# Eighteen places instead of ten for the feed-forward pieces between the attention groups of a unit

## The reference, cut to what matters

```
q, k = l2norm(LN(x) @ w_q), l2norm(LN(x) @ w_k);  v = x @ w_v
m    = (0.5 + 0.5 tanh(15 (q k' - 0.27))) * gate_q * gate_k      # no softmax: a sigmoid of the scores
x1   = LN(x + (m @ v) @ w_o + b_o)
h    = silu(Q(x1) @ Q(w_gate)') * (Q(x1) @ Q(w_up)')             # Q: blockwise FP4 grid, 704 columns
out  = LN(x1 + Q(h) @ Q(w_down)')
```

## Time and profile before

| | |
|---|---|
| median of 3 runs | 4472.55 us (4470.05 to 4476.02) |
| the profiled execution | 4469.53 us, its span 4467.7 us |
| PE busy / ACT busy / DVE busy | 93% / 90% / 35% of the span |
| granted TensorE clock | 0.985 of 2.4 GHz over the span, 1.00 in the main stage's stretches shown |

### The profile page before, as it was taken

One profiled execution on the slowest core, in us unless ns is written; L12 is line 12 of the kernel. 1 busy time (PEld: TensorE's weight loads), 2 busy tenths in 40 slices (PEclk: granted clock), 3 DMA queues, 4 the chain that ended last, 5 costly groups with the idle time before them and its releaser, 6 DMA issues.

```text
span 4467.7 us, 80907 instructions
## 1 busy us (share of the span) xinstructions
PE 4139.1 (93%) x28776; PEld 1293.7 (29%) x28776; DVE 1558.9 (35%) x4536; ACT 4026.8 (90%) x3275; POOL 159.2 (4%) x120
## 2 busy tenths in 40 slices
PE   7977889999999999999999999999999999999997
PEld 5651222222222222222222222222222222222223
DVE  6772013233333323332333332333233333333235
ACT  4658999999999999999999999999999999999993
POOL 2330000000000000000000000000000000000001
PEclk9989999999999999999999999999999999999998
DMA  3445433443344434443344334433444344434440
GB/s 110 125 116 83 61 61 61 76 76 60 57 75 77 64 61 67 77 67 62 63 77 70 61 62 77 77 60 61 72 77 64 63 66 76 72 57 64 77 80 14
DMA packets 180059, 315.51 MB, mean 71 GB/s; under 512 B 65265, under 2 KB 141809, under 8 KB 154609
## 3 DMA queue, kind: packets, MB, share of 16 engines
q1 hardware_dynamic: 179568, 309.41, 41.2%
HBM read 266.82 MB, written 42.47 MB: 69 GB/s over the span
## 4 chain that ended last, share of the span: by engine, by line
PE 68%; ACT 16%; issue 8%; DVE 4%; DMA 2%; SPq 2%; POOL 0%; ACTq 0%; POOLq 0%; DVEq 0%
PE ps L1213 34%; PE ps L1203 19%; ACT room L660 15%; PE ps L1240 7%; PE ps L1263 4%; DMA m_f<-fused_t 1%; DVE room L807 1%; SPq L486 1%; PE ps L1158 0%; SPq L462 0%; DVE st L761 0%; DMA vt<-v_gated 0%; DVE xnT L797 0%; PE ps L1225 0%; PE ps L1169 0%
## 5 line engine op out<-in xcount | busy, mean ns | idle before, releaser
L660 ACT ACTIVATE room<-ps 128x1024 f32<-128x1024 f32 (+1 forms) x2816 | 3792.9, 1416 | 246.2 <-PE ps L1203 231.7
L1213 PE MATMUL ps<-room,vt 128*32 128x512 f32 x16384 | 2064.4, 605 | 0.0
L1203 PE MATMUL ps<-qs,room 64*128 64x512 f16 x8198 | 1330.5, 384 | 249.5 <-ACT room L660 214.3
L1203 PEld LDWEIGHTS ps<-qs,room 64*128 64x128 f16 x8198 | 311.2, 93 | 1802.3 <-ACT room L660 1133.9
L1213 PEld LDWEIGHTS ps<-room,vt 128*32 128x32 f32 x16384 | 389.7, 109 | 954.8 <-issue 954.8
L1240 PE MATMUL ps<-wguT,m_xqT 128*128 128x352 f32 x960 | 348.2, 485 | 0.0
L905 DVE TENSOR_TENSOR vz<-ps,vz 128x352 f32<-128x352 f32 x120 | 63.0, 525 | 757.7 <-ACT vz L665 757.7
L910 DVE TENSOR_TENSOR vz<-ps,vz 128x352 f32<-128x352 f32 x120 | 63.0, 525 | 595.9 <-PE ps L1240 595.9
L1263 PE MATMUL ps<-wdnT,wqk 128*128 128x256 f32 x720 | 198.9, 404 | 0.6 <-DVE wqk L875 0.6
L1240 PEld LDWEIGHTS ps<-wguT,m_xqT 128*128 128x128 f32 x960 | 162.6, 189 | 105.2 <-issue 54.3
L561 POOL TENSOR_TENSOR m_x<-m_x,bo 128x256 f32<-128x256 f32 x60 | 43.6, 727 | 3972.7 <-DMA m_x<-in_L_attn_x_dram 3972.7
(11 more groups left out here) (165 smaller groups left out, 2211.0 us busy)
## 6 DMA issues: line engine op xcount, KB each, us to landing
room<-k_parts SPq DMA_DIRECT2D x520, 256.0 KB, 9.8
vt<-v_gated SPq DMA_DIRECT2D x65, 1024.0 KB, 17.5
qs<-q_parts SPq DMA_DIRECT2D x520, 32.0 KB, 10.4
gqb<-q_gates SPq DMA_DIRECT2D x256, 64.0 KB, 2.1
room<-in_L_attn_x_dram SPq DMA_DIRECT2D x16, 512.0 KB, 4.2
v_gated<-vz SPq DMA_DIRECT2D x64, 128.0 KB, 2.1
q_parts<-room SPq DMA_DIRECT2D x32, 256.0 KB, 2.1
k_parts<-room SPq DMA_DIRECT2D x32, 256.0 KB, 2.2
```

Source lines behind the costliest of these rows:

```text
L660: act.activation(res[:, c, o:o + m, :], ps[:, o:o + m, :], ACT.Sigmoid, scale=2 * SHARP / QK_UP ** 2, bias=-2 * SHARP * THRESH).then_inc(b ...
L1203: ins = pe.matmul(ps[:, BANK[n % 2] + i, :], ks[o:o + HROWS, par, h // 2, kt * P:(kt + 1) * P], qs[o:o + HROWS, par, h // 2, :], start=Tru ...
L1213: ins = pe.matmul(ps[32 * h:32 * h + 32, SUM_BANK, :], vt[:, par, n * HD:n * HD + 32], r, start=kt == 0, stop=kt == KT - 1, skip_group_che ...
```

## The change

The tables name eighteen places where they named ten. P becomes P0 and P1 (places 5 and 6, before 7), X moves from 19 to 18, each of G0 to G3 becomes two single products (21 and 22, 26 and 27, 30 and 31, 34 and 35, before 23, 27, 31, 35), and D0 and D1 become D0, D1, D2, D3 and D45 (9, 10, 11, 13 and 14, before 11 and 15). H0 and H1 stay. ACT's two sigmoids of the gates come behind groups 24 and 28, before 25 and 29. The waits go with the first product of what was a piece, the signals with the last one.

```diff
-BEGIN = {7: "P", 19: "X", 23: "G0", 27: "G1", 31: "G2", 35: "G3"}
-END = {0: "H0", 3: "H1", 11: "D0", 15: "D1"}
-GATE_ACT = {25: 0, 29: 1}
+BEGIN = {5: "P0", 6: "P1", 18: "X", 21: "G0", 22: "G1", 26: "G2", 27: "G3", 30: "G4", 31: "G5", 34: "G6", 35: "G7"}
+END = {0: "H0", 3: "H1", 9: "D0", 10: "D1", 11: "D2", 13: "D3", 14: "D45"}
+GATE_ACT = {24: 0, 28: 1}
...
-                if what == "P":
-                    pe.wait_ge(l_f, 16 * (k + 1))
-                    wait(pe, l_hT, 2 * k)
-                    for c in range(DC):
-                        ins = pe.matmul(c_ps[:, 0:D], m_f[:, c, :], wo[:, c, :], start=c == 0, stop=c == DC - 1)
-                    ins.then_inc(l_P, 1)
+                if what[0] == "P":
+                    c = int(what[1])
+                    if c == 0:
+                        pe.wait_ge(l_f, 16 * (k + 1))
+                        wait(pe, l_hT, 2 * k)
+                    ins = pe.matmul(c_ps[:, 0:D], m_f[:, c, :], wo[:, c, :], start=c == 0, stop=c == DC - 1)
+                    if c == DC - 1:
+                        ins.then_inc(l_P, 1)
...
-                    p = int(what[1])
-                    if p == 0:
+                    p, c = divmod(int(what[1]), DC)
+                    if p == 0 and c == 0:
                         pe.wait_ge(l_xT, k + 1)
-                    else:
+                    elif c == 0:
                         pe.wait_ge(l_ge, 4 * k + p)
-                    for c in range(DC):
-                        ins = pe.matmul(c_ps[:, 0:FH], m_xqT[:, c, :], wguT[:, c, p * FH:(p + 1) * FH],
-                                        start=c == 0, stop=c == DC - 1)
-                    ins.then_inc(l_G, 1)
+                    ins = pe.matmul(c_ps[:, 0:FH], m_xqT[:, c, :], wguT[:, c, p * FH:(p + 1) * FH],
+                                    start=c == 0, stop=c == DC - 1)
+                    if c == DC - 1:
+                        ins.then_inc(l_G, 1)
...
-                    half = int(what[1])
-                    if half == 0:
+                    steps = [int(i) for i in what[1:]]
+                    if steps[0] == 0:
                         pe.wait_ge(l_hT, 2 * k + 2)
...
-                    for j in range(3 * half, 3 * half + 3):
+                    for j in steps:
...
-                    if half == 1:
+                    if steps[-1] == FT_FULL:
                         ins.then_inc(l_D, 1)
```

## The result

The changed kernel takes 4679.9 us (median of 4) against 4473.5 for the one before: 1.0468 times as long, 95% interval 1.0444 to 1.0493, or 209 us more (ratio less one, times 4470, as everywhere below). The profiled execution took 4678.25 us, its span 4676.4: 208.7 more than the one of before. The forecast was 4682, of which 216 us were the change.

A forecast was written before the change was run, and what follows sets the result against it. PE was taken as the bound wherever pieces stand, ACT elsewhere. D +43, X 0, P +81 and G +104 add to 228, together +216 by the walk; 4469.5 + 216 = 4685.5, named as 4682, range 4580 to 4722.

The forecast's parts named there:

- The walk: One unit carried through its 44 places with timings from the profile: 62.2 us for the kernel before, +216 for the change.
- The bound: PE bounds the kernel wherever pieces stand, ACT where none do, the two coupled by the two-group lead.
- The split's 0.20 us: Each division of a G, D or P piece adds 0.20 us on PE; eight splits make 1.6 us per unit.
- The upper price: Pieces at even places, behind sums, keep entry and exit as beside scores: 0.53 us to the piece, 0.39 at its end.
- Rival 1: Sums and pieces run into each other without a seam, saving 0.20 us at each of eight places: 4616, chance 0.25.
- m_f: P0 at place 5 newly waits for the m_f transfer, taken as 1.0 us mean; P's edit alone +81 us.
- The sigmoid behind 28: ACT's gate sigmoid waits for G3, so ACT stands 1.1 us ahead of group 29, of which 0.4 stays in the sum.
- D: Down projection pieces spread over five places: +43 us by the upper price, 36 of it from three splits.
- G: Gate pieces spread over eight places: +104 us with the sigmoids behind 24 and 28, 48 of it from four splits.
- Faster (3): Spreading halves ACT's idle time: 4370; needs splits under about 0.05 us, m_f ahead of place 5, no ACT wait for G3; chance 0.05.
- Nothing to see (4): Added costs stay inside PE's idle time at the scores, 2.9 us per unit, so no change shows; chance 0.03.
- The further wait (2): Another new wait, most likely G0 at 21 for the copy of X: 4715 with 0.5 us more per unit; chance 0.08.

The follow-up runs named there:

- v_places: Kernel before with H1 at 1, D as three pairs at 11, 15 and 18, X at 20, gate sigmoids behind 26 and 30: 4411.4 us, ratio 0.9872.

## Why the prediction was right

- **The sum.** +216 forecast, +209 measured (1.0444 to 1.0493, 198 to 220 us). That the 4682 lies 2 us from the measured 4679.9 is partly luck: the sum gave 4685.5 from the profiled execution, which lay 3 us below the median, so the step to a median is up, to 4688.5, and not down to 4682. Another part cancels inside the sum. The walk describes the ordinary unit and was taken times sixty, 3.6 us each. In the two profiles three units of four grew by 3.7 us on average and the fourth, which is longer in every kernel, by 3.0.
- **The bound.** PE's order of work and the two-group lead set the time. Table edits that neither add nor remove an instruction moved it from -57 to +209 us.
- **The split's 0.20 us.** Single pieces take 0.79 to 0.80 us (foreseen 0.79), and a cycle 6.05 for 5.85. Four splits on odd places cost 51 us (48, with the order 53).
- **Behind sums.** The upper price was right: the last instruction of the sums starts at 2038.26, the piece 0.52 behind it (foreseen 0.53), where passes inside the sums are 0.43 apart. Rival 1 (4616) falls with the row at 2038.78. What the Trainium skill states on draining (TensorEngine Tiling (Array Packing), Tiling Modes, Key Properties) agrees with it: the four-strip sums and a full product are seamed by the same 0.10 us as sums and scores.
- **m_f.** 47 units wait, 54.0 us in all, which is 0.9 for each of sixty units and 1.15 for each that waits. I had a mean of 1.0 over all units in the sum, and some 45 units of about 1 us among the signs; these two don't agree, and the measured value lies between them. The edit of P costs 74 us by its undoing and I had 81 alone or 69 taken back from the changed kernel. P at 5 whole had 96 and measured 88.
- **The sigmoid behind 28.** 1.08 us against 1.1 us (0.91 as the profile counts idle time), and 23 us of time against 26 (17 with P back at 7), so the larger part of that wait did lie beside PE's bound.
- **D.** 42 against 43. **G** with the sigmoids 95 against 104 alone, 103 as taken back.
- **What came out otherwise.** P divided over 6 and 7 costs nothing (+1, 0.9992 to 1.0013) and not 8. The walk let most of that split count and took in some waiting for m_f at place 6; but ACT bounds the stretch behind P, and the wait is as long as before (5.4 us in 8 units of 3000 us, 5.7 before). So "PE is the bound wherever pieces stand" was too wide: beside P it is ACT. And the ordinary unit takes 66.2 us, a little over the 65 to 66 named.
- **Rivals.** Faster (3) needed all three of its conditions and had none. Nothing to see (4): in the whole of 209 us PE's idle time at the scores didn't take up the added work; it grew. The further wait (2) didn't come: PE has no idle time ahead of G's products (0.0 us by the page of the changed kernel), so X's copy is in time. That the chance stood mostly on one mechanism was fair: a recurrence that gives 62.2 for a measured 62.3 to 62.4 priced the twelve later kernels within 11 us each.

Open: why every fourth unit, the first of the loop's body, takes up to 5 us longer than the others in all kernels, by the steps between gate sigmoids. The runs don't touch it. X at 18 alone, G at the changed places without any other edit, and H1 and the sigmoids of v_places each alone, weren't run.

## What to carry to other kernels

Where two engines alternate with a fixed lead, carry one period place by place from the rows of the profile; if it gives the measured period, it prices every other order before it is built. Dividing a filler piece costs an entry and an exit each time. Here it paid where it carried part of the work to a stretch in which PE idles (a third D piece, -27 us), was free where the other engine was the bound (P over 6 and 7, +1), and cost where PE was (D +42, G on odd places +51). And before a consumer is moved up, look at which issues stand on the queue ahead of what it reads: here four loads that nobody needed before the end of the unit cost 57 us.

## What the runs showed of the hardware

A seam between TensorE's three shapes of use (scores on two row halves, sums on four column strips, full products) costs about 0.10 us (0.52 for 0.43 behind sums, 0.39 for 0.295 behind a gate product), also where both are float32 and use all 128 rows (the piece at 2038.78). The first instruction of a piece takes another 0.10 (0.40 for 0.295), and the two make the 0.20 of a split. Inside a piece the instructions follow at 0.295 us for 352 columns, from one product to the next as well. Nine issues on SP, about half a microsecond apart, put the issue of m_f 5.4 us behind the first of them (2057.38 to 2062.77), more than twice the 2.4 us (median) that the transfer takes to land. Without the four gate loads among them it is 3.4 us.
